# Two changes around GpSimd's queue in a two-layer graph network: how the output is scattered, and how often the ring of layer 1 is waited for

## The reference

```python
h = jnp.maximum(_layernorm(x), 0.0)
x = x + relu(h @ W_self + mean(h[src] over dst) @ W_neigh + b)
h = jnp.maximum(_layernorm(x), 0.0)
xs = h[src]
hid = relu(concat([xs, h[dst]]) @ We1 + be1)
e = sigmoid(hid @ We2 + be2)
m = e * xs
messages = concat([segment_max(m, dst), segment_sum(m, dst)])
h2 = relu(concat([messages, h]) @ Wn1 + bn1)
x = x + h2 @ Wn2 + bn2 + h
```

## Time and profile before

| what | value |
|---|---|
| median of 3 runs | 5259.38 us (5255.86 to 5267.56) |
| the profiled execution | 5262.5 us, its span 5260.8 us |
| busy share of the span | PE 39%, DVE 76%, ACT 53%, POOL 69% |
| ring of layer 1: gathers on POOL | 2144, mean 961 ns |
| output: scatters on POOL | 98, mean 995 ns |
| granted TensorE clock in the ring | 0.50 |

### The profile page before, as it was taken

How to read it: one execution, slowest core, us unless ns; L and a number is a source line. 1 busy time by engine, 2 the same in 40 slices (tenths; PEclk the granted TensorE clock), 3 DMA queues, 4 the chain that set the end, 5 groups by cost and what they waited for, 6 DMA issues and landing times.

```text
span 5260.8 us, 105391 instructions
## 1 busy us (share of the span) xinstructions
PE 2050.8 (39%) x18339; PEld 1792.9 (34%) x18339; DVE 4010.2 (76%) x8532; ACT 2784.6 (53%) x7311; POOL 3653.6 (69%) x3826
## 2 busy tenths in 40 slices
PE   0208889999999999000111111111111111111110
PEld 0107788888888888000111111111111111111110
DVE  7787888888888887004888888888888888888870
ACT  7407677878888787002444444444544444444440
POOL 5627027777777777776777777777777777777777
PEclk9958999999999999555555555555555555555555
DMA  7441335554555555555444444444444444444451
GB/s 224 113 77 39 36 88 169 160 157 153 165 163 163 161 162 158 160 156 117 124 133 132 129 135 135 135 136 136 135 130 133 136 133 135 135 136 134 135 109 26
DMA packets 491280, 696.11 MB, mean 132 GB/s; under 512 B 249885, under 2 KB 339843, under 8 KB 491163
## 3 DMA queue, kind: packets, MB, share of 16 engines
q0 software_dynamic: 181472, 381.28, 27.2%
q1 hardware_dynamic: 228085, 172.05, 10.8%
q10 hardware_dynamic: 81638, 141.95, 8.1%
HBM read 513.68 MB, written 163.18 MB: 129 GB/s over the span
## 4 chain that ended last, share of the span: by engine, by line
PE 23%; DVE 20%; issue 20%; POOL 13%; DMA 9%; ACT 8%; ACTq 5%; DVEq 3%; POOLq 0%; SPq 0%
PE ps_acc L1934 11%; PE ps L1926 9%; POOL counts_f L581 7%; DVE act_w L1475 5%; POOL extra_f L581 4%; DMA counts_f<-early_rows 4%; ACT counts_f L1668 3%; DMA counts_f<-hA_table,stage 3%; DVE run_max L1492 3%; DVE pre L1469 2%; ACT msg L1767 2%; DVE z L1481 2%; ACTq L1767 1%; POOL out_dram L717 1%; DVEq L1469 1%
## 5 line engine op out<-in xcount | busy, mean ns | idle before, releaser
L581 POOL DMA_INDIRECT counts_f<-hA_table,stage x2144 | 2060.4, 961 | 681.8 <-issue 626.0
L1668 ACT ACTIVATE counts_f<-ps 128x784 bf16<-128x784 f32 x1568 | 1270.5, 824 | 509.2 <-PE ps L1926 425.3
L581 POOL DMA_INDIRECT extra_f<-hA_table,estage x984 | 932.7, 948 | 314.6 <-issue 291.6
L1469 DVE TENSOR_TENSOR pre<-counts_f,ps 128x512 f32 (+1 forms) x862 | 588.4, 683 | 669.7 <-ACT ps L1752 277.1
L1767 ACT ACTIVATE msg<-counts_f,gate (+1 forms) x3448 | 921.5, 337 | 315.8 <-ACT gate L1762 286.3
L1934 PE MATMUL ps_acc<-pieces_f,counts_f 128*128 128x192 bf16 x9604 | 1021.6, 247 | 2.2 <-issue 2.2
L1934 PEld LDWEIGHTS ps_acc<-pieces_f,counts_f 128*128 128x128 bf16 x9604 | 886.1, 138 | 2.9 <-issue 2.5
L1926 PE MATMUL ps<-hot 128*128 128x196 bf16 x6272 | 820.8, 253 | 132.4 <-ACT counts_f L1668 108.6
L2005 PE MATMUL ps_acc<-ident,h_tile 128*64 128x128 f32 x98 | 38.6, 394 | 2065.1 <-DVE cat L1528 2065.1
L1762 ACT ACTIVATE gate<-z,be_col (+1 forms) x862 | 256.2, 297 | 1022.6 <-DVE z L1481 662.7
L2005 PEld LDWEIGHTS ps_acc<-ident,h_tile 128*64 128x64 f32 x98 | 12.7, 129 | 2081.2 <-issue 2081.2
(11 more groups left out here) (252 smaller groups left out, 2875.6 us busy)
## 6 DMA issues: line engine op xcount, KB each, us to landing
early_rows<-extra_f SPq DMA_DIRECT2D x294, 384.0 KB
counts_f<-early_rows ACTq DMA_DIRECT2D x98, 1152.0 KB
counts_f<-hA_table,stage POOLq DMA_INDIRECT x2144
counts_f<-counts_f SPq DMA_DIRECT2D x67, 288.0 KB
extra_f<-hA_table,estage POOLq DMA_INDIRECT x984
own<-own_rows ACTq DMA_DIRECT2D x98, 130.0 KB
hA_table<-node ACTq DMA_DIRECT2D x98, 96.0 KB
ranked_rows<-zeros SPq DMA_DIRECT2D x1, 3724.0 KB, 38.7
```

The source lines that it names most:

```text
L581: return pool.indirect_dma_start(to, None, table, bass.IndirectOffsetOnAxis(ap=idx, axis=axis))
L1469: v.tensor_tensor(pre[:, :, :], rows[:, :, D:WROW], ps_b[:, bass.ds(i & 1, 1), :].to_broadcast([P, SLOTS, H]), ALU.add).then_inc(s_pre, 1)
L1668: act.activation(counts[:, c, nodes, :].rearrange("p (b h) t -> p b (h t)", h=2), ps_pairs[g & 1][:, :].rearrange("p (b w) -> p b w", b=BA ...
```

## The change

Two things are changed. In the ring, POOL waits ahead of the even chunks only, and there for the eight places of this chunk and the next. For the output, the staging copies of DVE and their two buffers go; POOL scatters each tile straight from `out_ranked` with the numbers in `ranked`, in 98 written-out steps, each waiting for its tile's `s_finished` count, with one semaphore for all.

```diff
@@ gather_layer (POOL)
                         for c in range(STAGE_CHUNKS * h, STAGE_CHUNKS * (h + 1)):
 
-                            wait_alone(pool, ly.used, g * GROUP_COLS + (c + 1) * SLOTS)
+                            if c % 2 == 0:
+                                wait_alone(pool, ly.used, g * GROUP_COLS + (c + 2) * SLOTS)
                             for s in range(SLOTS):
@@ POOL, after gather_layer
-            with in_one_block(pool, 0, TITER) as it:
-                for h in range(2):
-                    wait_alone(pool, s_outs, 4 * it + 2 * h + 2)
-                    for k in range(THALF):
-                        pool.indirect_dma_start(
-                            out[:, :], bass.IndirectOffsetOnAxis(ap=out_idx[:, h, k, 0:1], axis=0),
-                            out_rows[:, h, k, :], None, bounds_check=N - 1,
-                            oob_is_err=False).then_inc(s_outw[h], 16)
-            for h in range(2):
-                pool.wait_ge(s_outw[h], 16 * THALF * TITER)
+            pool.wait_ge(s_words, 16)
+            for t in range(T):
+                pool.wait_ge(s_finished, t + 2)
+                pool.indirect_dma_start(
+                    out[:, :], bass.IndirectOffsetOnAxis(ap=ranked[:, t, 0:1], axis=0), out_ranked[:, t, :], None,
+                    bounds_check=N - 1, oob_is_err=False).then_inc(s_outw, 16)
+            pool.wait_ge(s_outw, 16 * T)
@@ DVE, around the last tile
-            def stage_out(tiles_at, h):
-                v.tensor_copy(out_rows[:, h, :, :], out_ranked[:, tiles_at, :]).then_inc(s_outs, 1)
-                v.tensor_copy(out_idx[:, h, :, :], ranked[:, tiles_at, 0:2]).then_inc(s_outs, 1)
-
-            wait_alone(v, s_dve, st.now())
-            wait_alone(v, s_finished, T - 1)
-            wait_alone(v, s_words, 16)
-            for h in range(2):
-                stage_out(slice(h * THALF, (h + 1) * THALF), h)
             tile(T - 1, T - 2, None)
...
-            wait_alone(v, s_finished, T + 1)
-            with in_one_block(v, 0, TITER - 1) as it:
-                for h in range(2):
-                    wait_alone(v, s_outw[h], 16 * THALF * (it + 1))
-                    stage_out(bass.ds(it * (2 * THALF) + (2 + h) * THALF, THALF), h)
```

More of the change, by code:

```diff
@@ L276, in gnn_kernel @@
         tstage = sb("tstage", [P, 2, THALF, 2], I32)
-        out_rows = sb("out_rows", [P, 2, THALF, D])
         runs = sb("runs", [P, 2, THALF, RUN], I32)
@@ L343, in gnn_kernel @@
         early = counts_f[:, RING_END:RING_END + 2 * EROW].rearrange("p (k w) -> p k w", w=WROW)
-        out_idx = tstage
         ps_4 = psum("ps_4", [P, 4 * BANK])
@@ L482, in gnn_kernel @@
         s_hids = sem("s_hids")
-        s_outs = sem("s_outs")
-        s_outw = [sem(f"s_outw{h}") for h in range(2)]
+        s_outw = sem("s_outw")
         def tile_word(eng, i, at, low, high):
```

## The result

Over 22 runs of each on the same chips the changed kernel takes 5265.9 us in the median, the kernel before 5259.9; the ratio is 1.0013, with a 95% interval of 1.0007 to 1.0019. So it is slower, by some 4 to 10 us; the 6.0 us between the medians are less than half of the 15.5 us forecast. The time is inside the range, but outside the forecast's own 5270 to 5282, and inside the 0.2% that I called no change (chance 0.24, against 0.72 for slower). The ratio leaves out one far slower execution of each kernel.

What follows compares the result with a forecast made beforehand. POOL was taken as the bound from 2402 us to the end. Span 5260.8 + 16.8 - 1.3 = 5276.3 us, 5278.0 with 1.7 around it; against the runs' median 5274.9 us, 0.3% slower, range 5262 to 5288.

Steps and rivals of the forecast that it cites:

- The bound and the place: From 2402 us POOL sets the end; longer pauses at some ten even-chunk starts, 2500 to 3050 us, together near 24.5 us.
- The first waits: Ring, first tiles: POOL's lateness is 4.1 us at gather 81, 5.0 at 89, 4.1 at 137, 8.8 at 177.
- The output: Scatters after the ring: DVE's copies go, 0.013 us for each of 98 scatters, 1.3 us less.
- Waits as instructions: Ring: the 268 removed waits with their increments cost nothing, since POOL's queue handles them under the gather before.
- Term one, +16.8 us: Ring's even chunks: waiting for four places more makes POOL late, carried place by place through DVE to +16.8 us.
- absorbed: Rival, ring: DVE makes up its lateness in waits for early rows; +5.0 - 1.3, 5263.1 us; chance 0.13.
- the adding one: Rival, ring: DVE is as late as POOL every time, all shortfalls add; +53 - 1.3, 5311 us; chance 0.06.
- DVE's waits: Ring, 2510 to 3145 us: DVE's waits for landed places rise above 0.5 us.
- The test that I had set: Wrong if POOL's pauses sum to under 18 us, or if a scatter's step isn't near 1.285 us.
- The bounds: Ring's lateness: at least 5.0 us if DVE never became late, at most +53 us if always as late as POOL.

Runs made afterwards that it cites:

- the dose with sixteen places: Against the kernel before, POOL waits for sixteen free places ahead of every fourth chunk, output staged as before: 5390.9 us, ratio 1.0251.

## Why the prediction was right, and where its size was off

**The bound and the place.** Right. POOL sets the end; longer pauses of it, nearly all at the firsts of even chunks in the first tiles, are what the change costs. The ring's change alone costs no less than the whole, and the dose with sixteen places moves the time by its pauses.

**The first waits.** Right for gather 81, and somewhat too high for the next ones: gather 81 was to start 4.1 us late and paused 4.06 us longer; gather 89 was to pause 1.7 us longer than the common pause and did so by 1.15; gather 177, forecast 4.7, did so by 3.8.

**The output.** Right: -1.3 us forecast, -0.9 and -1.2 in the two profiles that have it. By the Trainium skill ("SBUF — State Buffer", the warning on DVE blocking DMAs issued by GpSimd) it would have been 4.7 by my estimate. The trace doesn't bear that size out: the eleven scatters that began under a copy were 0.09 to 0.13 us longer, with 0.22 to 0.26 us of the copy still to run, and that tenth of a us a copy was all there was to give back.

**Waits as instructions.** Right at nothing, and shown by the run with four times as many of them in the ring.

**Term one, +16.8 us: the step whose size was wrong.** Its pauses gained 5.1 us in the changed kernel's profile and 10.5 in that of the ring's change alone; the timed difference is 6 us, and 9 in that experiment. The step was "POOL's 5.0 us make DVE 1.2 us late. All later reports move with DVE", carried on place by place: the lateness of DVE was off from the third place on, and I had DVE keep what it once had. For it I let each chunk's rows land as long after its last gather as they had in the kernel before. That time doesn't belong to the chunk. In the kernel before, the chunk of gathers 225 to 228 had a long one; POOL's gathers, ACT's load of early rows, SP's copy of the ring's first places (line 888), and its report, in the kernel before:

```profile
2690.47 0.62 ACTq L1734 DMA_DIRECT2D counts_f<-early_rows  x1
...
2693.51 1.17 POOL L581 DMA_INDIRECT counts_f<-hA_table,stage  x1 [0.30 <-issue]
...
2698.31 0.53 SPq L888 DMA_DIRECT2D counts_f<-counts_f  x1
...
L891 SPq EVENT_SEMAPHORE  x2: 17/17/17, 2701.1 to 2701.9; - x2
```

and in the changed one, where the chunk's last gather began at 2700.80:

```profile
2692.39 0.62 ACTq L1714 DMA_DIRECT2D counts_f<-early_rows  x1
...
2700.80 0.95 POOL L578 DMA_INDIRECT counts_f<-hA_table,stage  x1 [0.30 <-issue]
...
2703.47 0.52 SPq L883 DMA_DIRECT2D counts_f<-counts_f  x1
...
L886 SPq EVENT_SEMAPHORE  x1: 17/17/17, 2706.1 to 2706.1; - x1
```

Before, the gather ended at 2694.7, 4 us after ACT had issued its load of early rows; the copy could be issued 3.6 us later, the report came 6.4 us after the gather. In the changed kernel POOL was 7.3 us later, and the load's last packet had ended at 2697.9, ahead of the gather's end at 2701.75: 1.7 us to the copy, 4.4 to the report. DVE began this chunk at 2706.42 instead of 2701.40. Of these 5.0 us 1.4 were there at 2500 us already, before any longer wait, so 3.6 come from the waits (my working had 6.2). Over the whole ring of the kernel before, the report follows the last gather by 1.72 us in the median of the 364 plain chunks beside no load of early rows, and by 3.18 in that of the 105 beside one (a load issued in the 6 us before the gather's end or just behind it; drawn wider or narrower, 2.8 to 3.5); for the first chunks of groups, with the copy, 4.36 (48) and 6.51 (19). The changed kernel has the same: 1.71 and 3.34, 4.35 and 6.78. Which chunk meets the load moves with POOL's own lateness.

How much of the error this explains I worked out by carrying the lateness again over the rows of before, with the landing times of the later profiles put in: +8.9 us with the changed kernel's and +9.4 with the ring-only kernel's instead of 16.8, and 142 instead of 188 for sixteen places (127 measured). With the landing times of the two profiles in which POOL isn't made late (the output's change alone, and a wait for each place) the same working gives 19 and 14, which speaks against mere chance; but such a number is good to a few us only.

The "absorbed" rival had a part in it too: DVE gave lateness back at its waits for early rows. In the changed kernel it waited for landed rows at 2665 us and became late by that, and at its next wait for early rows it made up for most of it:

```profile
2665.58 0.69 DVE L1464 TENSOR_TENSOR pre<-counts_f,ps 128x512 f32 x1 [1.46 <-SPq L886]
...
2674.52 0.69 DVE L1464 TENSOR_TENSOR pre<-counts_f,ps 128x512 f32 x1 [5.94 <-DMA counts_f<-early_rows]
```

The same two chunks in the kernel before:

```profile
2662.07 0.67 DVE L1469 TENSOR_TENSOR pre<-counts_f,ps 128x512 f32 x1
...
2672.74 0.69 DVE L1469 TENSOR_TENSOR pre<-counts_f,ps 128x512 f32 x1 [7.68 <-DMA counts_f<-early_rows]
```

It was 3.5 us later at the first and 1.8 at the second, with 1.4 of either there from 2500 us on. All its waits for early rows went from 148.6 us before to 142.6, and to 129.1 with sixteen places (146.7 with the ring's change alone). That the landing times are the larger part is worked out from the traces, not shown by a run of its own. I had priced the absorbed case at +3.7 us and the adding one at +52; the measured 6 lies nearer to the absorbed case than to my forecast, and the range holds it only because it reached down toward that rival.

**DVE's waits.** The forecast had those for landed places from 2510 to 3145 us rise above 0.5 us. They did:

```profile
DVE pre L1464 <- DMA counts_f<-early_rows: 59.9, 11, 8.2
...
DVE pre L1464 <- SPq L886: 8.0, 6, 3.6
```

**The test that I had set.** "Wrong if the pauses sum to under 18 us": 12.8 in this profile and 18.2 in the other. By my own test the size was wrong, and the match of the profiled span hid it: the missing 11.7 us of pauses were made up by 10.5 us of longer gathers, and the median of the timed runs is 12.5 us below this profiled one. The bounds were sound; the forecast's own range, 5270 to 5282, was not. It varied DVE's times and left the landings where they were.

## What to carry to other kernels

Coarsening a wait on a ring saved nothing here, where a satisfied wait cost nothing, and it asks for as many more free places as it coarsens by; it costs where the ring runs full, and that can be read from before by setting each start against the report that it would then need. Lateness carried over from such a reading came out too high in both doses (16.8 us for 5 to 10, 188 for 127): landing times moved with what else was in flight, and the consumer gave lateness back at waits of another kind. For differences of a few us, split a profile into its terms before believing that its total agrees.

## What was unexpected of the hardware

The time from a 96 KB gather's end to the report of its landing nearly doubles, 1.72 to 3.18 us in the median, beside a load of 1,152 KB from another queue. A gather's own length on POOL varies between 0.94 and 1.23 us, and the sum of 2,144 of them by 17 us from profile to profile of nearly the same program; in the six profiles every gather over 1.07 us began beside a `TENSOR_TENSOR` of DVE on `run_max` or `run_sum`. And two chips took 45 and 47% longer for the kernel before. In the kernels profiled there some 1,600 to 1,800 of 38,000 queue instructions of ACT, DVE and SP take 0.6 to 0.8 us, where the median is 0.04; the kernel before has none such on the first kind of chip. On these two the coarser waits cost 0.7 to 1.8% for parts of the ring which on the others cost 0.16% as a whole.
